# A post-norm attention and channel-mix block: GpSimd's bias sum split per block, and every engine's step in another order

## The chip, the cores and the metric

The kernel runs on one core of a Trainium2 chip. The metric is the device time of one execution in microseconds, taken from repeated runs; the profile is one execution recorded by the hardware profiler. The engines are named PE (TensorE, matrix products and transposes), DVE (VectorE), ACT (ScalarE), POOL (GpSimd) and SP (SyncE, here only the queue that issues DMAs). Each runs its own instructions strictly in the order of the program and waits on semaphores that the others raise.

## The reference

One sequence of 4096 tokens of 256 features goes through two layers, each followed by a layer norm without gain:

```python
# attention: 16 heads of 16 features, 4 key/value groups, each query sees itself and the 127 tokens before it
q = x @ Wq + bq;  k = x @ Wk + bk;  v = x @ Wv + bv          # k, v: 4 groups x 16
scores = where(i - 128 >= j or i < j, -1e9, q @ k.T / sqrt(16))
x = layernorm(x + softmax(scores) @ v @ Wo + bo)
# channel mix: every token is mixed with the one before it
xr = mu_r * x + (1 - mu_r) * x_prev;  xk = mu_k * x + (1 - mu_k) * x_prev
x = layernorm(x + sigmoid(xr @ W_r.T) * (relu(xk @ W_k.T) ** 2 @ W_v.T))
```

## The kernel before

The tokens are cut into 32 blocks of 128, and four blocks make a superblock (8 of them). Projections are made per superblock: three chunks of 128 columns (chunk 0 holds k and v, chunks 1 and 2 hold q; L893), split by ACT, DVE and POOL into three bf16 parts (high, middle, low: L517, L528, L402; rest: L677), spilled to DRAM by SP and loaded back with the parts stacked along the contraction (ks, qs: L312 to L329). v is turned by four transposes (L908) and copied to vals (L686).

The rest goes by blocks. For block t+1, DVE copies qs to query tiles (tile_q, L696), PE computes scores of tiles only to find their row maxima (six groups, "max 0 to 5", L943 and L952), DVE reduces them (L704), casts and transposes them (turn_max, L711 to L718), and SP writes them into two extra rows of qs (L336), so that the real scores come out with the maximum taken off. For block t, PE makes eight score products of 128x512 ("score 0 to 7", L969) into two PSUM banks, ACT takes their exponentials (L535), POOL zeroes what the window excludes (mask, L410). PE multiplies by the values (L983), turns the result back (L1040), DVE normalises (L808, L814), PE turns it again (L1048) and applies Wo (output product, L1081). DVE adds x + bo from x_bo and takes the moments (first residual, L830, L723 to L728), POOL raises the variance to -1/2 and forms the shift (root, L417, L419), ACT applies the norm (L582). PE turns x2 (L1032), ACT copies it (L592), POOL forms the difference of neighbouring tokens (L470), DVE makes two pairs of mixes (L780), PE the r product (L1059) and the k product (L1070), ACT tanh, relu and square (L598, L603, L609), PE the second product (L1024), DVE the gate (L789) and the second residual with its moments (L799), POOL the second root, ACT the second norm (L617), SP the store (L342).

All this is a software pipeline: in step t (block j = t mod 4 of superblock s) each engine works on several blocks at once, in an order written out by hand in its function `step`, which `run` calls. In step t, PE computes the maxima of t+1, the scores of t, the values and attention transposes of t-1, the output product and turn of x2 of t-2, the r and k products of t-3, the second product of t-4. Projections of superblock s+2 begin in the step with j = 3 (chunks 0 and 1) and go on as those of s+1 in the steps with j = 0 (chunk 2) and j = 1 (turn of v).

x_bo holds x + bo for two superblocks. It is made by POOL from x_in, loaded by SP, in one instruction per superblock of 128x1024 elements (L396), for superblocks 2 to 7 in the step with j = 2, between masks 2 and 3:

```python
                nc.gpsimd.tensor_tensor(x_bo[:, par], x_in[:, par],
                                        bo_b.unsqueeze(1).to_broadcast([P, SB_BLKS, D]), ALU.add).then_inc(s_xbo, 1)
```

## Time and profile before

| | us |
|---|---|
| median of 3 runs | 454.38 (453.68 to 455.26) |
| the profiled execution, its own time: the span from its first to its last instruction | 449.1 |
| TensorE busy in it | 407.7 |
| VectorE busy | 344.6 |
| ScalarE busy | 272.8 |
| GpSimd busy | 291.2 |

The busy times are sums of the durations of one engine's instructions, so an engine at 91% may still not be the cause of the other 9%. The span is that of one recorded execution; the runs are timed apart from it, from outside, and come out a few microseconds longer. DMA runs beside all this on 16 engines and moves 39.25 MB.

### The profile page before, as it was taken

The page shows a single profiled execution, that of the slowest core. Times are in us where ns is not written, and L with a number is a line of the kernel's source. Part 1 is how long each engine was busy: PE and PEld are TensorE (multiplying, and loading weights), DVE is VectorE, ACT ScalarE, POOL GpSimd, SP SyncE. Part 2 cuts the span into 40 slices and gives each one's busy share as a digit, 9 for nine tenths or more (in the row PEclk, how much of TensorE's full clock was granted, in tenths as well). Part 3 has the DMA queues.
Part 4 walks back from the last instruction along what each step waited for, and adds up shares of the span by engine and source line. Part 5 has one row for each costly group of instructions (what it writes and reads, how often), then busy time and mean ns, then how long its engine had stood idle before and what let it go on. Part 6 is the DMA issues. An engine that isn't in the chain of part 4 may idle for free.

```text
span 449.1 us, 8432 instructions
## 1 busy us (share of the span) xinstructions
PE 407.7 (91%) x2542; PEld 251.9 (56%) x2542; DVE 344.6 (77%) x852; ACT 272.8 (61%) x566; POOL 291.2 (65%) x466
## 2 busy tenths in 40 slices
PE   8976999997999979997999979997999979999853
PEld 3444546664556656564556665564656656665532
DVE  5765775898678976899688986799878988996551
ACT  2512567775667747764677657666577657778522
POOL 4552666776487856677487766688487767876531
PEclk9986899998999989999999989999999989999995
DMA  8484585412733175321753146421823144000000
GB/s 324 115 141 91 134 148 138 100 49 46 140 101 84 50 94 146 82 66 43 110 163 86 49 74 152 87 60 47 120 65 94 49 62 70 14 13 27 12 23 23
DMA packets 50892, 39.25 MB, mean 87 GB/s; under 512 B 33696, under 2 KB 42400, under 8 KB 50720
## 3 DMA queue, kind: packets, MB, share of 16 engines
q1 hardware_dynamic: 50416, 37.93, 38.9%
q10 hardware_dynamic: 432, 0.79, 0.6%
q8 instruction: 20, 0.33, 0.3%
q14 instruction: 24, 0.20, 0.2%
HBM read 26.38 MB, written 12.06 MB: 86 GB/s over the span
## 4 chain that ended last, share of the span: by engine, by line
PE 64%; DVE 19%; ACT 6%; issue 6%; DMA 2%; POOL 1%; SPq 1%; ACTq 0%; DVEq 0%; POOLq 0%
PE av_ps L983 11%; PE score_ps L969 9%; PE proj_ps L893 8%; PE max_ps L952 6%; PE gen L1070 6%; PE gen L1024 6%; PE gen L1081 5%; PE gen L1059 4%; DVE neg_max L704 4%; DVE q_tiles L696 3%; DVE max_parts L711 3%; PE max_ps L943 3%; ACT parts L517 2%; DVE mix L780 2%; PE av_ps L1040 2%
## 5 line engine op out<-in xcount | busy, mean ns | idle before, releaser
L410 POOL TENSOR_SCALAR_AFFINE_SELECT probs<-probs 128x512 f32<-128x512 f32 x252 | 168.2, 678 | 108.0 <-ACT probs L535 105.7
L535 ACT ACTIVATE probs<-score_ps 128x512 f32<-128x512 f32 x252 | 148.4, 598 | 86.0 <-PE score_ps L969 85.6
L969 PE MATMUL score_ps<-qs,ks 98*128 98x512 bf16 x252 | 99.8, 398 | 2.2 <-ACT probs L535 1.4
L704 DVE TENSOR_REDUCE neg_max<-max_ps 128x3 f32<-128x480 f32 x144 | 87.4, 631 | 12.3 <-PE max_ps L952 12.1
L983 PE MATMUL av_ps<-probs,vals 128*32 128x512 f32 x504 | 67.0, 605 | 0.9 <-POOL probs L410 0.8
L969 PEld LDWEIGHTS score_ps<-qs,ks 98*128 98x128 bf16 x252 | 25.0, 100 | 57.3 <-ACT probs L535 47.9
L1070 PE MATMUL gen<-mix,rest_w 128*128 128x128 f32 x256 | 38.7, 299 | 16.9 <-DVE mix L780 15.5
L952 PE MATMUL max_ps<-ks,q_tiles 96*128 96x160 bf16 x416 | 52.3, 243 | 0.0
L417 POOL TENSOR_TENSOR rstd<-var,minus_half 128x1 f32<-128x1 f32 x64 | 35.7, 558 | 21.7 <-DVE var L728 20.8
L1070 PEld LDWEIGHTS gen<-mix,rest_w 128*128 128x128 f32 x256 | 35.4, 208 | 22.7 <-DVE mix L780 17.8
L780 DVE SCALAR_TENSOR_TENSOR mix<-diff,first,x_t 128x128 f32<-128x128 f32 x128 | 43.8, 385 | 0.0
L952 PEld LDWEIGHTS max_ps<-ks,q_tiles 96*128 96x128 bf16 x416 | 37.9, 103 | 8.2 <-issue 1.9
L677 DVE SCALAR_TENSOR_TENSOR rest<-proj_ps,first,parts 128x512 f32<-128x512 f32 x19 | 14.3, 751 | 35.5 <-ACT parts L517 32.4
L893 PE MATMUL proj_ps<-x_t,first 128*128 128x512 f32 x76 | 38.3, 628 | 0.7 <-DMA first<-w_first 0.7
L943 PE MATMUL max_ps<-edge_mask,ident_b 128*128 128x192 bf16 x138 | 35.2, 255 | 3.2 <-issue 2.1
L1024 PE MATMUL gen<-rest_w,act_k 128*128 128x256 f32 x128 | 35.9, 405 | 2.1 <-ACT act_k L609 2.0
L402 POOL TENSOR_TENSOR parts<-rest,parts 128x512 bf16<-128x512 f32 x24 | 30.7, 1282 | 10.5 <-ACT parts L528 10.5
L1059 PE MATMUL gen<-rest_w,mix 128*128 128x256 f32 x128 | 34.3, 390 | 3.0 <-DVE mix L780 3.0
L1081 PE MATMUL gen<-rest_w,att_c 128*128 128x256 f32 x128 | 32.9, 379 | 0.0
L696 DVE COPY q_tiles<-qs 96x2048 bf16<-96x2048 bf16 x32 | 27.3, 853 | 5.0 <-DMA qs<-q_parts 5.0
L603 ACT ACTIVATE relu_k<-gen 128x256 f32<-128x256 f32 x32 | 12.7, 397 | 29.8 <-PE gen L1070 29.8
L582 ACT ACTIVATE x<-y,shift,rstd 128x256 f32<-128x256 f32 x32 | 19.2, 599 | 17.4 <-POOL shift L419 16.6
(86 smaller groups left out, 663.2 us busy)
## 6 DMA issues: line engine op xcount, KB each, us to landing
qs<-q_parts SPq DMA_DIRECT2D x48, 192.0 KB, 6.1
q_parts<-parts SPq DMA_DIRECT2D x48, 128.0 KB, 2.2
x_t<-x_feat SPq DMA_DIRECT2D x8, 512.0 KB, 3.7
x_in<-x_nat SPq DMA_DIRECT2D x8, 512.0 KB, 4.5
out<-out_t SPq DMA_DIRECT2D x32, 128.0 KB, 2.0
ks<-k_parts SPq DMA_DIRECT2D x42, 80.0 KB, 2.9
qs<-q_parts SPq DMA_DIRECT2D x42, 64.0 KB, 2.2
k_parts<-parts SPq DMA_DIRECT2D x8, 192.0 KB, 2.8
```

Source lines behind the costliest of these rows:

```text
L410: nc.gpsimd.affine_select(out=v, in_=v, compare_op=ALU.is_ge if i % 2 else ALU.is_gt, fill=0.0, base=0, pattern=[[0, HPG], [sign, BLK]], c ...
L535: nc.scalar.activation(probs[:, buf, i], score_ps[i % 2][:, :], ACT.Exp, scale=SCALE).then_inc(s_exp, 1)
L704: nc.vector.tensor_reduce(neg_max[:, TPB * i:TPB * i + n], max_bank(t, j, i)[:, 0:n * TILE_KEYS].rearrange("p (n k) -> p n k", k=TILE_KEYS ...
L780: nc.vector.scalar_tensor_tensor(out=mix[:, w, c], in0=diff[:, c], scalar=small_cols[:, MU_COL + w * DC + c:MU_COL + w * DC + c + 1], in1= ...
L893: ins = nc.tensor.matmul((ps or proj_ps)[:, 0:SB], wqkv[:, c, m * P:(m + 1) * P], x_t[:, par, c], start=(c == 0), stop=(c == DC - 1))
L952: ins = nc.tensor.matmul(dst, q_tiles[:, j % 2, tile], ks[0:ROWS, par, g, k0:k0 + TILE_KEYS], start=False, stop=(k == len(tiles) - 1), ski ...
L969: nc.tensor.matmul(score_ps[i % 2][:, :].rearrange("p (h q) -> p h q", q=BLK), ks[0:ROWS + MPARTS, par, g, k0:k0 + BLK], qs[0:ROWS + MPART ...
L983: ins = nc.tensor.matmul(av_ps[g * VCOL:(g + 1) * VCOL, :], vals[:, pk, jk, g, :], probs[:, j % 2, 2 * g + half], start=(half == 0 or not ...
L1024: ins = nc.tensor.matmul(gen0[:, 0:D], act_k[:, c], w_t[:, 2, c], start=(c == 0), stop=(c == DC - 1))
L1059: ins = nc.tensor.matmul(gen0[:, 0:D], mix[:, 0, c], w_t[:, 0, c], start=(c == 0), stop=(c == DC - 1))
L1070: ins = nc.tensor.matmul(gen0[:, o * BLK:(o + 1) * BLK], w_t[:, 1, c, o * P:(o + 1) * P], mix[:, 1, c], start=(c == 0), stop=(c == DC - 1))
L1081: ins = nc.tensor.matmul(gen1[:, 0:D], att_c[:, c], wo[:, c], start=(c == 0), stop=(c == DC - 1))
```

## The change

The sum of x and bo is made per block, in 128x256 elements, one a step, into a ring of four blocks (x_bo[:, t % 4]). It waits until the first residual of the block four before has read its place, and the load of x_in waits for the sums of its superblock's blocks. `run`, `superblock` and the `step` functions are replaced by one loop over t for each engine, unrolled for all 32 blocks and a few steps of drain, with the same operations in another order; `on(u)` is true for blocks that exist, `ahead(u)` where u is the first block of a superblock from 2 on (or from 1 on). The waits between operations are the same or follow from the new order (tanh, square and tile_q have one more wait each, on things done long before; PE's waits for free PSUM banks are written anew). The small tensors of the two norms are put together in pairs.

```diff
-        x_bo = sb("x_bo", [P, 2, SB_BLKS, D])
+        x_bo = sb("x_bo", [P, 4, D])
...
@@ sync: the loop (the start issues the same transfers as before)
+            for t in range(NBLK + 6):
+                if on(t - 6):
+                    store(t - 6)
+                if ahead(t + 1, 1):
+                    stack_q((t + 1) // SB_BLKS, 1, SB_BLKS, s_stack)
+                if ahead(t + 4, 1):
+                    spill_k((t + 4) // SB_BLKS)
+                if ahead(t + 2, 1):
+                    stack_q((t + 2) // SB_BLKS, 0, 1, s_stack0)
+                if ahead(t + 5):
+                    load_nat((t + 5) // SB_BLKS)
+                if ahead(t + 6):
+                    load_feat((t + 6) // SB_BLKS)
+                if ahead(t + 4, 1):
+                    stack_k((t + 4) // SB_BLKS)
+                if 1 <= t + 1 < NBLK:
+                    max_in(t + 1)
+                if ahead(t + 4, 1):
+                    spill_q((t + 4) // SB_BLKS, 0)
+                    spill_q((t + 4) // SB_BLKS, 1)
...
@@ gpsimd
-            def x_plus_bo(s, par):
-                if later(s, 2):
-                    pool.wait_ge(s_y1, (s - 1) * SB_BLKS)
-                pool.wait_ge(s_x[par], loaded(s, par))
-                nc.gpsimd.tensor_tensor(x_bo[:, par], x_in[:, par],
-                                        bo_b.unsqueeze(1).to_broadcast([P, SB_BLKS, D]), ALU.add).then_inc(s_xbo, 1)
+        def _(pool):
+            def x_plus_bo(t):
+                if t >= 4:
+                    pool.wait_ge(s_y1, t - 4 + 1)
+                pool.wait_ge(s_x[t // SB_BLKS % 2], loaded(t // SB_BLKS))
+                nc.gpsimd.tensor_tensor(x_bo[:, t % 4], x_in[:, t // SB_BLKS % 2, t % SB_BLKS], bo_b,
+                                        ALU.add).then_inc(s_xbo, 1)
...
+            for t in range(NBLK + 5):
+                if on(t - 1):
+                    mask(t - 1, 7)
+                if on(t - 3):
+                    difference(t - 3)
+                if on(t - 5):
+                    root(t - 5, 1)
+                if 2 <= t + 1 < NBLK:
+                    x_plus_bo(t + 1)
+                if ahead(t + 3):
+                    low_part((t + 3) // SB_BLKS, 2)
+                if on(t):
+                    mask(t, 0)
+                if on(t - 2):
+                    root(t - 2, 0)
+                if on(t):
+                    mask(t, 3)
+                    mask(t, 2)
+                    mask(t, 1)
+                    mask(t, 4)
+                if ahead(t + 5):
+                    low_part((t + 5) // SB_BLKS, 0)
+                if ahead(t + 4):
+                    low_part((t + 4) // SB_BLKS, 1)
+                if on(t):
+                    mask(t, 5)
+                    mask(t, 6)
@@ scalar: the loop
+            for t in range(NBLK + 5):
+                if on(t - 2):
+                    att_c_copy(t - 2)
+                if on(t - 1):
+                    exps(t - 1, 7)
+                if on(t):
+                    exps(t, 0)
+                if ahead(t + 5):
+                    high_part((t + 5) // SB_BLKS, 0)
+                if ahead(t + 3):
+                    middle_part((t + 3) // SB_BLKS, 2)
+                if on(t):
+                    exps(t, 1)
+                    exps(t, 2)
+                if ahead(t + 4):
+                    middle_part((t + 4) // SB_BLKS, 1)
+                if on(t - 5):
+                    second_norm(t - 5)
+                if on(t - 1):
+                    att_t_copy(t - 1)
+                if on(t - 3):
+                    tanh(t - 3)
+                if on(t):
+                    exps(t, 3)
+                if on(t - 2):
+                    first_norm(t - 2)
+                if on(t):
+                    exps(t, 4)
+                if ahead(t + 4):
+                    high_part((t + 4) // SB_BLKS, 2)
+                if ahead(t + 5):
+                    middle_part((t + 5) // SB_BLKS, 0)
+                if on(t - 3):
+                    relu(t - 3)
+                if on(t):
+                    exps(t, 5)
+                if on(t - 3):
+                    square(t - 3)
+                if ahead(t + 5):
+                    high_part((t + 5) // SB_BLKS, 1)
+                if on(t):
+                    exps(t, 6)
+                if on(t - 2):
+                    x2_t_copy(t - 2)
@@ vector: the loop
+            for t in range(-1, NBLK + 5):
+                if 1 <= t + 1 < NBLK:
+                    tile_max(t + 1, 1)
+                if on(t - 5):
+                    second_moments(t - 5)
+                if 1 <= t + 1 < NBLK:
+                    tile_max(t + 1, 2)
+                    tile_max(t + 1, 3)
+                if on(t - 3):
+                    mixed(t - 3, 0)
+                if 1 <= t + 1 < NBLK:
+                    tile_max(t + 1, 4)
+                if on(t - 4):
+                    gate(t - 4)
+                if on(t - 2):
+                    first_residual(t - 2)
+                    token_before(t - 2)
+                if 1 <= t + 1 < NBLK:
+                    tile_max(t + 1, 5)
+                if on(t - 2):
+                    first_moments(t - 2)
+                if 1 <= t + 1 < NBLK:
+                    turn_max(t + 1)
+                if on(t - 3):
+                    mixed(t - 3, 1)
+                if on(t - 4):
+                    second_residual(t - 4)
+                if ahead(t + 5):
+                    rest_part((t + 5) // SB_BLKS, 0)
+                if 2 <= t + 2 < NBLK:
+                    tile_q(t + 2)
+                if on(t - 1):
+                    normalise(t - 1)
+                if ahead(t + 4):
+                    rest_part((t + 4) // SB_BLKS, 2)
+                if 1 <= t + 2 < NBLK:
+                    tile_max(t + 2, 0)
+                if ahead(t + 5):
+                    rest_part((t + 5) // SB_BLKS, 1)
+                if ahead(t + 3):
+                    val_copy((t + 3) // SB_BLKS)
@@ tensor: the loop
+            for t in range(NBLK + 4):
+                if ahead(t + 2):
+                    v_turn((t + 2) // SB_BLKS)
+                if on(t - 1):
+                    score(t - 1, 4)
+                if on(t - 2):
+                    turn_back(t - 2)
+                if ahead(t + 3):
+                    project_chunk((t + 3) // SB_BLKS, 2)
+                if on(t - 4):
+                    k_product(t - 4)
+                if on(t - 1):
+                    score(t - 1, 5)
+                if 1 <= t + 1 < NBLK:
+                    max_scores(t + 1, 0)
+                if ahead(t + 4):
+                    project_chunk((t + 4) // SB_BLKS, 1)
+                if 1 <= t + 1 < NBLK:
+                    max_scores(t + 1, 1)
+                if on(t - 3):
+                    turn_x2(t - 3)
+                if on(t - 1):
+                    score(t - 1, 6)
+                if on(t - 2):
+                    turn_attention(t - 2)
+                if on(t - 1):
+                    score(t - 1, 7)
+                if on(t - 4):
+                    second_product(t - 4)
+                if 1 <= t + 1 < NBLK:
+                    max_scores(t + 1, 2)
+                    max_scores(t + 1, 3)
+                if ahead(t + 5):
+                    project_chunk((t + 5) // SB_BLKS, 0)
+                if on(t):
+                    score(t, 0)
+                if on(t - 2):
+                    output_product(t - 2)
+                if 1 <= t + 1 < NBLK:
+                    max_scores(t + 1, 4)
+                if on(t):
+                    score(t, 1)
+                if 1 <= t + 1 < NBLK:
+                    max_scores(t + 1, 5)
+                if on(t):
+                    score(t, 2)
+                if on(t - 1):
+                    values(t - 1, 0)
+                    values(t - 1, 1)
+                if on(t - 3):
+                    r_product(t - 3)
+                if on(t):
+                    score(t, 3)
```

## Rows read from the trace of the kernel before

**Rows 1.** The page: busy us and share by engine; granted clock in 40 slices.

```profile
PE 407.7 (91%) x2542; PEld 251.9 (56%) x2542; DVE 344.6 (77%) x852; ACT 272.8 (61%) x566; POOL 291.2 (65%) x466
...
PEclk9986899998999989999999989999999989999995
```

**Rows 2.** Windows: stretch and length, busy us (instructions) by engine, clock, DMA.

```profile
378.88:388.80 9.92, 9.92 (x77) 6.79 (x75) 9.08 (x26) 7.63 (x18) 7.73 (x13) 1.00 0.05 14
...
215.61:229.62 14.01, 13.90 (x86) 8.18 (x83) 9.84 (x27) 9.51 (x21) 8.98 (x16) 1.00 0.66 143
...
229.62:241.97 12.35, 12.05 (x81) 7.32 (x79) 10.28 (x24) 8.89 (x20) 8.78 (x14) 1.00 0.42 90
...
241.97:252.61 10.64, 10.64 (x81) 7.23 (x79) 9.78 (x27) 7.19 (x16) 8.17 (x14) 1.00 0.24 61
...
252.61:267.10 14.49, 11.78 (x78) 7.88 (x75) 12.53 (x30) 8.14 (x20) 9.89 (x15) 0.88 0.28 62
...
304.12:317.17 13.05, 10.36 (x77) 6.62 (x75) 12.43 (x30) 7.62 (x18) 9.55 (x14) 1.00 0.21 52
...
97.34:368.89 271.55, 253.14 (x1638) 159.85 (x1635) 224.68 (x555) 178.55 (x375) 190.66 (x296) 0.97 0.41 87
```

**Rows 3.** Timeline, 256 to 268 us: start, us, instruction, [idle before, releaser].

```profile
258.86 2.36 POOL L396 TENSOR_TENSOR x_bo<-x_in,rest_w 128x1024 f32<-128x1024 f32 x1
...
258.97 2.29 DVE L711 CAST max_parts<-neg_max 128x16 bf16<-128x16 f32 x1
...
263.23 2.07 PE L1070 MATMUL gen<-mix,rest_w 128*128 128x128 f32 x8 [2.58 <-DVE mix L780]
```

**Rows 4.** Single lines: count, duration in ns min/median/max, first and last start.

```profile
L396 POOL TENSOR_TENSOR x_bo<-x_in,rest_w x8: 2347/2355/2362, 16.8 to 360.4; 128x1024 f32<-128x1024 f32 x8
...
L470 POOL TENSOR_TENSOR diff<-x_t x32: 607/612/613, 61.6 to 434.5; 128x256 f32<-128x256 f32 x32
...
L711 DVE CAST max_parts<-neg_max x32: 178/240/2285, 32.5 to 404.8; 128x16 bf16<-128x16 f32 x32
...
L799 DVE SCALAR_TENSOR_TENSOR y<-gated,x x32: 414/844/1375, 86.0 to 444.1; 128x256 f32<-128x256 f32 x32
```

**Rows 5.** Timeline, 282 to 300 us: GpSimd and VectorE at once.

```profile
285.16 1.16 POOL L402 TENSOR_TENSOR parts<-rest,parts 128x512 bf16<-128x512 f32 x1
...
285.18 0.65 DVE L704 TENSOR_REDUCE neg_max<-max_ps 128x3 f32<-128x480 f32 x1
```

**Rows 6.** Timeline, 372 to 386 us: statistics, norm, and what follows it.

```profile
382.12 0.43 DVE L723 BATCH_NORM_STATS2 stats<-y 128x6 f32<-128x256 f32 x1
...
384.19 0.60 ACT L582 ACTIVATE x<-y,shift,rstd 128x256 f32<-128x256 f32 x1
...
384.70 0.56 ACT L567 COPY att_t<-av_ps 128x512 f32<-128x512 f32 x1
```

**Rows 7.** Groups of the whole span: busy us, mean ns | idle before, releaser.

```profile
L410 POOL TENSOR_SCALAR_AFFINE_SELECT probs<-probs 128x512 f32<-128x512 f32 x252 | 168.2, 678 | 108.0 <-ACT probs L535 105.7
...
L535 ACT ACTIVATE probs<-score_ps 128x512 f32<-128x512 f32 x252 | 148.4, 598 | 86.0 <-PE score_ps L969 85.6
...
L704 DVE TENSOR_REDUCE neg_max<-max_ps 128x3 f32<-128x480 f32 x144 | 87.4, 631 | 12.3 <-PE max_ps L952 12.1
...
L780 DVE SCALAR_TENSOR_TENSOR mix<-diff,first,x_t 128x128 f32<-128x128 f32 x128 | 43.8, 385 | 0.0
...
L609 ACT ACTIVATE act_k<-relu_k 128x256 f32<-128x256 f32 x32 | 13.3, 417 | 1.0
...
L572 ACT COPY att_c<-av_ps 128x256 f32<-128x256 f32 x32 | 11.6, 364 | 0.0
```

**Rows 8.** The chain that ended last, in order: start, us, what.

```profile
272.84 1.93 PE proj_ps L893 x4
```

**Rows 9.** Issues of the q stack for blocks 1 to 3, and their landing.

```profile
L327 SPq DMA_DIRECT2D qs<-q_parts x90: 302/428/1258, 25.8 to 367.4; - x90
...
DMA to landing us min/median/max: 2.1/3.7/8.9
```

More of the change, by code:

```diff
@@ L381, in tail @@
-            def tail():
-                for buf in range(2):
-                    sp.wait_ge(s_store[buf], 16 * (NBLK // 2) + 1)
-                    sp.nop(nofuse=True)
-            run(sp, start, step, tail)
+                sp.dma_start(out_blk[t], out_t[:, t % 2]).then_inc(s_store[t % 2], 16)
+            load_feat(0)
+            load_nat(0)
+            sp.dma_start(rest_w[:, :], w_rest).then_inc(s_restw, 16)
+            load_feat(1)
+            load_nat(1)
+            spill_k(0)
+            spill_q(0, 0)
@@ L870, in _ @@
-            run(dve, start, step)
+            zeros()
+            identities()
+            rest_part(0, 0)
+            rest_part(0, 1)
+            rest_part(0, 2)
+            val_copy(0)
+            masks()
+            rest_part(1, 0)
+            rest_part(1, 1)
+            rest_part(1, 2)
+            val_copy(1)
+            tile_q(0)
+            tile_max(0, 0)
+            tile_max(0, 1)
+            tile_max(0, 2)
+            tile_max(0, 3)
+            tile_max(0, 4)
+            tile_max(0, 5)
@@ new lines, in turn_attention, with r_product @@
+            def turn_attention(t):
+                pe.wait_ge(s_att, t + 1)
+                for c in range(DC):
+                    ins = nc.tensor.transpose(av_ps[:, c * BLK:(c + 1) * BLK], att[:, c * P:(c + 1) * P],
+                                              ident[:, :])
+                ins.then_inc(s_ctr, 1)
+            def r_product(t):
+                pe.wait_ge(s_mix, t * 4 + 2)
+                if t:
+                    pe.wait_ge(s_gated, t)
+                for c in range(DC):
+                    ins = nc.tensor.matmul(gen0[:, 0:D], mix[:, 0, c], w_t[:, 0, c], start=(c == 0),
+                                           stop=(c == DC - 1))
+                ins.then_inc(s_r, 1)
@@ new lines, in k_product, with output_product @@
+            def k_product(t):
+                pe.wait_ge(s_mix, t * 4 + 4)
+                pe.wait_ge(s_tanh, t + 1)
+                for o in range(DC):
+                    for c in range(DC):
+                        ins = nc.tensor.matmul(gen0[:, o * BLK:(o + 1) * BLK], w_t[:, 1, c, o * P:(o + 1) * P],
+                                               mix[:, 1, c], start=(c == 0), stop=(c == DC - 1))
+                ins.then_inc(s_k, 1)
+            def output_product(t):
+                pe.wait_ge(s_att_c, t + 1)
+                if t:
+                    pe.wait_ge(s_x2t, t)
+                for c in range(DC):
+                    ins = nc.tensor.matmul(gen1[:, 0:D], att_c[:, c], wo[:, c], start=(c == 0),
+                                           stop=(c == DC - 1))
+                ins.then_inc(s_wo_ps, 1)
```

912 lines of the change are left out of this document (350 added, 562 removed).

## The prediction

> **What bounds the kernel now.** I read the profiled execution, whose span is 449.1 us; the median of the runs shown, 454.4 us, stands 5.3 us above it, and those 5.3 us are added at the end. First the page's busy shares and its clock line: TensorE 91%, VectorE 77%, GpSimd 65%, ScalarE 61%, and a TensorE clock that is 9 nearly everywhere and dips to 8 now and then [rows 1]. 91% says "TensorE", the dips say "something stops it now and then", so the second view is the busy time step by step (from the start of one second product of the channel mix, L1024, to the next). The reader is to see three kinds of step [rows 2]. A plain step takes 9.92 us and TensorE is busy all of it, VectorE for 9.08, ScalarE for 7.63, GpSimd for 7.73. Steps with projection work take 14.01, 12.35 and 10.64 us, TensorE busy for all but 0.3 us at most. And the step with j = 2 takes 14.49 us although it has no projection work: TensorE is idle for 2.7 us of it and the granted clock falls to 0.88; one of them keeps its clock and takes 13.05.
>
> The third view, the timeline inside such a step, says why [rows 3]. GpSimd starts the sum of x and bo for a whole superblock (L396, 2.36 us) at 258.86. VectorE's next instruction is the cast of the row maxima (L711), started at 258.97, and it ends only when the sum does, after 2.29 us. Behind it in VectorE's order stand the rest of the maxima's transposition and the second pair of mixes, and the k product on TensorE waits for those, 2.58 us idle. Then TensorE starts at its lower level: eight pieces take 2.07 us. The cast takes 0.178 us at its shortest and 2.285 at its longest, the sum 2.35 us every time [rows 4].
>
> So: a pipeline at TensorE's 9.92 us a step, with one stop in each of six superblocks (1 to 6).
>
> **The sum of x and bo.** It goes from 8 instructions of 128x1024 to 32 of 128x256. The difference of neighbouring tokens (L470) is a GpSimd instruction of two operands of just that shape and takes 0.61 us [rows 4]. 4 x 0.61 = 2.44 us for a superblock against 2.36: nothing for GpSimd. What changes is the longest time for which it can hold VectorE up, 0.61 instead of 2.3 us. The stop's worth: the 21 steps from 97.34 to 368.89 are five of each projection kind and six with j = 2, 271.55 - 5 x (14.01 + 12.35 + 10.64) = 86.55; less 6 x 9.92 = 59.5 it is 27.0 us [rows 2]. If the small sums block nothing, all of it goes. Next late behind the k product would be TensorE's own queue, which is full, so no other wait takes the stop's place at once. Upper bound of what the small sums cost: each delays VectorE by 0.61 us and the delay goes whole to TensorE, in the 24 steps of the six superblocks, 14.6 us. Lower bound: 0. In the new order the sum stands behind the difference and the second root, when VectorE is about at a maximum from PSUM, the gate and the first residual. The nearest row is the low part of a projection (L402), on GpSimd over a maximum (L704): the maximum still takes 0.65 us [rows 5]. I take 0.
>
> The Trainium skill (SBUF — State Buffer, "Who interferes with whom") has it that the port pair that VectorE and GpSimd share is locked for a whole instruction, that the second to issue waits for all of it, and that VectorE's instructions with two SBUF inputs are hit as well as its fast copies and casts. The casts of 2.29 us agree. By that rule splitting frees no port time, and it speaks for the first rival below, which is priced from rows.
>
> **The order of the steps.** Counted through the loops, every engine issues what it issued before, so the busy times of a plain step stay. What moves: scores 4 to 7 of a block go over TensorE's step border, exponential 7 and mask 7 over those of ScalarE and GpSimd; on TensorE the transposes of the attention and of x2 and the k product go one step later; maximum 0 of the next block but one is taken at the end of VectorE's step. The question is whether the in-order queues still close in 9.9 us. The longest loop I find goes from one block's exponential 7 to the next one's: mask 7, the difference, the first pair of mixes, maximum 4, gate, first residual, maximum 5, the moments and the root, first norm, exponential 4, relu, exponential 5, square, exponential 6, the copies of x2 and of the attention, exponential 7. In numbers: four exponentials of 0.60 (2.40), the mask 0.68, the difference 0.61, two mixes of 0.385 (0.77), two maxima of 0.63 (1.26), six instructions of 256 columns (gate, residual, relu, square, two copies) of 0.36 to 0.42, at 0.40 (2.40), 2.07 from the start of the statistics to that of the norm, the norm 0.60 [rows 4, 6, 7]. Together 10.8 us. These are full durations; independent neighbours on an engine overlap: the norm of 384.19 takes 0.60 and the next one starts after 0.51 [rows 6]. With 0.09 us for each of 14 such neighbours the loop takes 9.5. Bounds 9.5 and 10.8 against TensorE's 9.92; I take 9.92, since the overlap has a row, so the cost is 0. The cover is thin, though: a first norm that waits now holds exponentials 4 and 5, and through them scores 6 and 7. At 10.8 the 27 steps from block 5 on would cost 0.88 x 27 = 24 us.
>
> In the steps with projection work the excess over 9.92 is 4.09 + 2.43 + 0.72 = 7.2 us a superblock. TensorE's own part are three chunks, the first of them 1.93 us and the others 1.7 [rows 8], and the turn of v, four transposes, 0.6: 6.0 us. The other 1.2 are waits for PSUM and for copies. In the new order the chunks start in three steps instead of two with more work between, and maxima 2 and 3 come behind scores and the second product instead of close behind 0 and 1. I take half back, 0.6 x 6 = 3.7 us; the ends are 0 and 7.5.
>
> **SyncE and its transfers.** Loads, stores, spills and stacks change places in SyncE's order. The tightest is the q stack of blocks 1 to 3, now behind the maxima's rows of block 3: six issues of 0.43 us, landing within 8.9 us at worst [rows 9], 11.5 us together, and the copy to q tiles that needs it stands some 13 us behind the first issue (one step of 9.9, the first chunk's 1.9, and about one more of the step before). Hidden, by 1.5 us. The second q spill of a superblock now waits for a low part one step later; queued behind it are a store and the next rows of maxima, which are due 1 to 2 us after: no cost.
>
> **Start and end.** The two big sums at the start shrink by 3.5 us together, but block 0 waits there for the q stacks: 0. The last 30 us are the chain of one block, with the same operations in the same sequence: 0, give or take 2.
>
> Sum: 449.1 - 27.0 - 3.7 = 418.4, and 5.3 make 423.7: **424 us**. This case's own range is 417 to 430 (projection waits 0 or 7.5 us back, thin cover 0 or 0.2 us a step).
>
> **Rivals.**
> 1. VectorE's block comes back in small: each new sum meets a cast, the copy of q tiles or an instruction of two SBUF operands. For it: the second residual (L799) takes 0.41 us at its shortest and 0.84 in the median [rows 4]. Against it: where the sum stands in the order, and the 0.84 us that VectorE has free in a plain step. Price 14.6 us: 439 us.
> 2. The loop rules, mildly: half-way between 9.92 and 10.8, 10.36 us a step, 12 us: 436 us. For it the sum of full durations, against it the overlap.
> 3. The loop rules and the kernel gets slower. One mechanism: the first norm of block t-2, which stands before exponential 4 on ScalarE, waits for GpSimd's first root, and that for VectorE's moments behind maximum 5, for which TensorE must have issued its maxima first; so scores 6 and 7 wait on late work of TensorE itself. It decides from the point where 27 steps lose the 30.7 us gained, 9.92 + 1.14 = 11.06 us a step. Full durations and 0.17 us of wait at three handoffs make 11.3: 27 x 1.38 = 37 us, 449.1 - 30.7 + 37.3 + 5.3 = 461 us. Against: today's step has nearly the same links and closes in 9.92.
> 4. TensorE isn't at its limit at 9.92, and a better order runs down to VectorE's 9.08 plus gaps, about 9.4: 27 x 0.5 = 14 us less, 410 us. For it: weight loads fill only 6.79 of the 9.92 us. Against it: no idle time at all [rows 2]. The Trainium skill (Perfetto Trace Analysis, "Identifying the Most-Contended Engine") calls matmul busy time a bad measure of the room left and asks for weight-load busy time; that rule is for this rival.
> 5. It doesn't do what it says: the big stop goes, but the q stack lands late instead, its 1.5 us of cover being gone; 3 us of wait and 1.5 of lower clock in six superblocks, 27 us: 451 us.
>
> **Chances.** Forecast 0.60, rival 1 0.13, rival 2 0.09, rival 3 0.09, rival 4 0.06, rival 5 0.03. About 0.3% is what a measurement of this kernel can tell from no change. Rivals 1, 2 and 4 are faster, rival 3 is slower, of rival 5 two thirds are no change; with a little for mishaps elsewhere: faster 0.87, same 0.03, slower 0.10. The range, 415 to 440, takes in the forecast and rivals 1 and 2, 0.82.
>
> **What would show it.** The cast's longest duration falls from 2.29 to under 0.8 us; 32 sums of about 0.61; no step of 13 to 15 us without projection work; TensorE busy 95% or more between the first and the last block, with no dips in the clock there; plain steps of 9.7 to 10.1 us. The prediction is wrong if plain steps take over 10.3 us with scores that wait for exponentials (rivals 2 and 3), if casts and q tile copies are long beside the new sums (rival 1), or if a copy to q tiles waits for a DMA (rival 5).

## The result

The changed kernel takes 412.5 us (median of 4 executions, 409.1 to 413.4) against 454.6 us for the kernel before (453.7 to 455.3): a ratio of 0.908, 95% interval 0.901 to 0.914. The direction was forecast, the size was not: 424.0 us and the range of 415 to 440 both lie above it. In a later job the two had a ratio of 0.913 (0.895 to 0.930). Medians and ranges in this document hold every execution; ratios leave out those that stand over 1.5% above the fastest of their kernel.

**The profile after.** The page first: busy us and share by engine, the clock line, and the shares of the chain of work that ended last.

```profile
PE 382.1 (93%) x2542; PEld 247.2 (60%) x2542; DVE 304.3 (74%) x852; ACT 268.7 (65%) x566; POOL 295.6 (72%) x490
...
PEclk9997799999999999999999999999999998999998
...
PE 56%; DMA 17%; DVE 10%; SPq 7%; issue 4%; ACT 3%; POOL 2%; ACTq 0%; POOLq 0%; DVEq 0%
```

The dips of [rows 1] in the middle of the clock line are gone. New is "DMA 17%" in the chain (2% before): a transfer is now part of what sets the end. VectorE's busy time fell by 40 us with the same 852 instructions; the cast (19.3 us in all before, 7.3 now) and the second residual (25.3 and 13.4) are 24 of them.

Windows by kind of step (from one second product of the channel mix, now L923, to the next; columns as in [rows 2]):

```profile
72.46:83.91 11.45, 11.45 (x80) 7.57 (x78) 10.01 (x25) 8.23 (x18) 7.96 (x12) 1.00 0.32 62
83.91:94.08 10.17, 10.17 (x79) 7.28 (x78) 8.67 (x27) 7.92 (x18) 9.56 (x16) 1.00 0.38 92
94.08:103.81 9.73, 9.73 (x75) 6.73 (x74) 8.95 (x28) 7.34 (x17) 7.99 (x15) 1.00 0.42 117
...
148.89:164.37 15.48, 13.41 (x83) 8.14 (x83) 9.30 (x27) 9.55 (x21) 10.70 (x17) 1.00 0.82 131
195.89:210.19 14.30, 13.41 (x83) 8.14 (x82) 9.50 (x27) 9.55 (x21) 10.61 (x17) 1.00 0.76 122
356.59:366.32 9.73, 9.73 (x76) 6.81 (x75) 8.36 (x26) 7.33 (x17) 8.36 (x15) 1.00 0.05 16
375.94:410.90 34.96, 24.87 (x139) 15.80 (x138) 16.50 (x57) 17.71 (x40) 16.62 (x34) 0.97 0.07 23
```

The step with j = 2 (third row) is now a plain step. Plain steps take 9.73 us, the stretch with chunk 2 of a projection 11.45 and the one with the turn of v 10.17 (before 12.35 and 10.64), TensorE busy all through. Chunks 0 and 1 both lie in the stretch from the second product of the step with j = 3 to the next, as before the change. Only that one did not get shorter: 13.72 to 15.48 us (before 14.01, one of them 14.48), with TensorE idle for up to 2.07 of them.

Single lines, as in [rows 4]: the small sum, the cast, the second residual, the copy of the q tiles.

```profile
L334 POOL TENSOR_TENSOR x_bo<-x_in,rest_w x32: 724/732/1071, 16.4 to 369.9; 128x256 f32<-128x256 f32 x32
...
L651 DVE CAST max_parts<-neg_max x32: 168/170/476, 30.3 to 372.2; 128x16 bf16<-128x16 f32 x32
...
L699 DVE SCALAR_TENSOR_TENSOR y<-gated,x x32: 417/418/426, 79.9 to 405.9; 128x256 f32<-128x256 f32 x32
...
L638 DVE COPY q_tiles<-qs x32: 645/683/1123, 25.2 to 363.6; 96x2048 bf16<-96x2048 bf16 x32
```

The cast's longest fell from 2.29 us to 0.48, the second residual from 0.84 in the median (1.38 at its longest) to 0.418, with 0.426 at its longest. The small sum takes 0.73 us, not the 0.61 of the forecast, so four of them are 2.93 us against 2.36 for the whole one.

Now the wait that came instead. VectorE's waits (us in total, times, longest), and the chain that ended last through one step with j = 3 (start, us, what):

```profile
DVE q_tiles L638 <- DMA qs<-q_parts: 16.2, 9, 5.6
```

```profile
147.56 1.48 SPq L274
...
149.09 0.42 SPq L274
...
150.97 9.16 DMA qs<-q_parts
...
160.16 0.93 DVE q_tiles L638
...
161.14 0.26 PE max_ps L875
```

SyncE issues the q stack of blocks 1 to 3 from 147.56 on, the last piece lands 12.6 us after that, and VectorE's copy, which had been free to start at 158.07, waits 2.09 us for it; TensorE's next maximum waits behind the copy.

**Where the 38.2 us of span went** (449.1 less 410.9), by stretches of equal work from the starts of the second products: the start, 1.9; the first two steps with projection work behind it, 1.4; the 21 steps of [rows 2]'s last row, 271.55 less 238.81 = 32.7 (six with j = 2: 27.4; ten with j = 0 and 1: 6.9; five with j = 3: 1.6 *lost*); the next four, 3.7 *lost* (12.93 and 10.77 among them, the last stack); everything from 375.94 on, 40.83 less 34.96 = 5.9.

### The profile page after: what moved, and what is told of

Read it like the earlier page. It is cut to its first block, busy times and chain, and to the rows that moved or that the text cites. A ratio compares the mean times of both kernels' runs of the same rounds, so it can differ in the third digit from the quotient of the medians.

```text
span 410.9 us, 8541 instructions
## 1 busy us (share of the span) xinstructions
PE 382.1 (93%) x2542; PEld 247.2 (60%) x2542; DVE 304.3 (74%) x852; ACT 268.7 (65%) x566; POOL 295.6 (72%) x490
## 4 chain that ended last, share of the span: by engine, by line
PE 56%; DMA 17%; DVE 10%; SPq 7%; issue 4%; ACT 3%; POOL 2%; ACTq 0%; POOLq 0%; DVEq 0%
DMA qs<-q_parts 15%; PE score_ps L901 8%; PE av_ps L914 7%; PE proj_ps L827 6%; PE max_ps L884 5%; PE gen L923 5%; PE gen L973 5%; SPq L274 4%; PE gen L954 4%; PE gen L963 4%; PE max_ps L875 2%; DVE neg_max L645 2%; SPq L282 2%; DVE q_tiles L638 2%; PE av_ps L937 2%
## 5 line engine op out<-in xcount | busy, mean ns | idle before, releaser
L350 POOL TENSOR_SCALAR_AFFINE_SELECT probs<-probs 128x512 f32<-128x512 f32 x252 | 162.2, 669 | 46.1 <-ACT probs L474 45.0
L901 PE MATMUL score_ps<-qs,ks 98*128 98x512 bf16 x252 | 91.7, 387 | 1.4 <-ACT probs L474 1.3
L914 PE MATMUL av_ps<-probs,vals 128*32 128x512 f32 x504 | 60.7, 598 | 0.3 <-POOL probs L350 0.2
L682 DVE SCALAR_TENSOR_TENSOR mix<-diff,first,x_t 128x128 f32<-128x128 f32 x128 | 40.7, 359 | 16.4 <-POOL diff L372 16.4
L954 PEld LDWEIGHTS gen<-rest_w,mix 128*128 128x128 f32 x128 | 21.7, 189 | 28.5 <-issue 24.3
L340 POOL TENSOR_TENSOR parts<-rest,parts 128x512 bf16<-128x512 f32 x24 | 28.7, 1199 | 11.7 <-ACT parts L465 11.7
L923 PE MATMUL gen<-rest_w,act_k 128*128 128x256 f32 x128 | 34.1, 389 | 1.8 <-ACT act_k L519 1.8
L963 PE MATMUL gen<-mix,rest_w 128*128 128x128 f32 x256 | 34.2, 276 | 1.6 <-DVE mix L682 0.9
L638 DVE COPY q_tiles<-qs 96x2048 bf16<-96x2048 bf16 x32 | 23.3, 729 | 16.2 <-DMA qs<-q_parts 16.2
L963 PEld LDWEIGHTS gen<-mix,rest_w 128*128 128x128 f32 x256 | 31.5, 191 | 5.7 <-issue 3.8
L360 POOL TENSOR_SCALAR shift<-mv,rstd 128x1 f32<-128x1 f32 x64 | 27.0, 421 | 6.3
```

The source lines that it names most:

```text
L350: nc.gpsimd.affine_select(out=v, in_=v, compare_op=ALU.is_ge if i % 2 else ALU.is_gt, fill=0.0, base=0, pattern=[[0, HPG], [sign, BLK]], c ...
L901: nc.tensor.matmul(score_ps[i % 2][:, :].rearrange("p (h q) -> p h q", q=BLK), ks[0:ROWS + MPARTS, s % 2, g, k0:k0 + BLK], qs[0:ROWS + MPA ...
L914: ins = nc.tensor.matmul(av_ps[g * VCOL:(g + 1) * VCOL, :], vals[:, b // SB_BLKS % 2, b % SB_BLKS, g, :], probs[:, t % 2, 2 * g + half], s ...
L923: ins = nc.tensor.matmul(gen0[:, 0:D], act_k[:, c], w_t[:, 2, c], start=(c == 0), stop=(c == DC - 1))
L954: ins = nc.tensor.matmul(gen0[:, 0:D], mix[:, 0, c], w_t[:, 0, c], start=(c == 0), stop=(c == DC - 1))
L963: ins = nc.tensor.matmul(gen0[:, o * BLK:(o + 1) * BLK], w_t[:, 1, c, o * P:(o + 1) * P], mix[:, 1, c], start=(c == 0), stop=(c == DC - 1))
```

## The experiments

**Was it the split or the order?** Three kernels. First the kernel before with nothing but the split, in the step with j = 2:

```diff
                 if ahead and j == 2:
-                    x_plus_bo(s + 1, 1 - par)
+                    x_plus_bo_block(s + 1, 1 - par, 0)
                 if scores:
                     mask(t, 3, j % 2)
+                if ahead and j == 2:
+                    x_plus_bo_block(s + 1, 1 - par, 1)
...
```

> The kernel before, with only the sum split: four sums of 128x256 instead of one of 128x1024, after masks 2, 3, 4 and 5 of the step with j = 2. Theory A (the length of one GpSimd instruction makes the stop): VectorE is held for 0.6 us at most at a time, most of the 27 us of the six stops goes, 428 to 433 us. Theory B (where the sum stands makes the stop, the port is held as long in all): the four sums meet the cast, the mixes and the copy of q tiles one after the other, 442 to 452 us.

Measured: 436.8 us (432.3 to 439.1), ratio 0.959 (0.949 to 0.969), between the two. The mechanism is theory B's, at a lower price: the small sums meet the cast, the mixes and the copy of the q tiles one after the other, and the cast and the copy are held up by 0.5 us each.

```profile
249.12 0.65 DVE L725 CAST max_parts<-neg_max 128x16 bf16<-128x16 f32 x1
...
252.05 0.72 POOL L403 TENSOR_TENSOR x_bo<-x_in,rest_w 128x256 f32<-128x256 f32 x1
252.13 1.20 DVE L710 COPY q_tiles<-qs 96x2048 bf16<-96x2048 bf16 x1
```

Then the kernel before with the whole sum, only moved:

```diff
-                if ahead and j == 2:
-                    x_plus_bo(s + 1, 1 - par)
                 if scores:
                     mask(t, 3, j % 2)
...
                 if f3:
                     difference(t - 3)
+                if ahead and j == 2:
+                    x_plus_bo(s + 1, 1 - par)
```

> The kernel before, with only the place of the big sum changed: from behind mask 2 to behind the difference, at the start of GpSimd's step. Theory A: the sum still holds VectorE for up to 2.3 us at its next instruction with two SBUF inputs or fast cast, and masks 0 and 1, the root and the first norm come 2.4 us late: 445 to 460 us. Theory B: VectorE is then at maxima, the gate and the first residual, which read PSUM; the cast is back at 0.2 us and 15 to 27 us go: 428 to 440 us.

Measured: 436.5 us (435.9 to 437.4), ratio 0.962 (0.954 to 0.969): the same gain without a split, and in the range of theory B. Last the new order with the sum whole again:

```diff
-                if 2 <= t + 1 < NBLK:
-                    x_plus_bo(t + 1)
+                if ahead(t + 1):
+                    x_plus_bo((t + 1) // SB_BLKS)
```

> The kernel after, with the sum of x and bo made whole again (128x1024, once a superblock, in the place of its first quarter). Theory A: the stop comes back, six times 4.5 us, 435 to 442 us. Theory B: in the new order the sum stands 3.4 us ahead of the cast, beside maxima, gate and residual from PSUM, and costs next to nothing: 411 to 417 us.

Measured: 408.5 us (407.5 to 410.3), ratio 0.902 (0.893 to 0.910), not slower than the change with its split (0.908): theory A is out. Windows of the step with j = 2 with the split alone and with the move alone:

```profile
242.77:254.10 11.33, 10.37 (x77) 6.63 (x75) 10.87 (x26) 7.64 (x18) 10.17 (x17) 1.00 0.25 63
```

```profile
98.38:110.32 11.94, 10.65 (x78) 6.58 (x75) 10.34 (x27) 7.41 (x18) 10.21 (x14) 1.00 0.29 66
```

and in the new order with the whole sum, the step with j = 3 that now holds it, the sum with its neighbours on VectorE, and the cast over the whole span:

```profile
237.33:251.06 13.73, 13.43 (x84) 8.15 (x83) 9.15 (x27) 9.56 (x21) 12.03 (x17) 1.00 0.80 135
```

```profile
240.90 2.36 POOL L333 TENSOR_TENSOR x_bo<-x_in,rest_w 128x1024 f32<-128x1024 f32 x1
242.12 0.66 DVE L644 TENSOR_REDUCE neg_max<-max_ps 128x3 f32<-128x480 f32 x1 [1.40 <-PE max_ps L883]
242.69 0.41 DVE L689 SCALAR_TENSOR_TENSOR gated<-tanh_r,gen 128x256 f32<-128x256 f32 x1
```

```profile
L650 DVE CAST max_parts<-neg_max x32: 168/170/409, 30.1 to 367.0; 128x16 bf16<-128x16 f32 x32
```

The reader is to see that the sum lasts 2.36 us as ever, and that VectorE meanwhile waits for TensorE and then takes a maximum and the gate out of PSUM, at their usual 0.66 and 0.41 us. So the stop was a matter of what stands beside the sum.

Splitting it or moving it each take more than half of it away in the old order: 14.5 us to 11.3 or 11.9, not to 9.9. About 1.5 us of that is clock (14.5 against the 13.05 of the step that kept it), which fell to 0.88 or 0.91 in five of these six steps before the change and is 1.00 in all of them in both experiments. What is left has two different causes. With the split it is the sums that VectorE still meets, shown above, and the step behind, with j = 3, grows from 14.01 to 14.66 in four of five cases. With the move the cast takes 0.18 us again, but GpSimd's own list is late: masks 0 and 1 and the first root stand behind the 2.36 us, the root starts 6.5 us into the step instead of 4.5, ScalarE's first norm waits for its shift, and TensorE for the copy behind the norm.

```profile
105.90 0.60 ACT L582 ACTIVATE x<-y,shift,rstd 128x256 f32<-128x256 f32 x1 [2.02 <-POOL shift L419]
...
107.02 0.66 PE L1040 MATMUL av_ps<-ident,att_t 128*128 128x128 f32 x4 [1.16 <-ACT att_t L567]
```

A long instruction on GpSimd thus has two prices, one at VectorE's next SBUF work and one in its own list. In the new order, where the whole sum falls into a step that has projection work for TensorE, neither shows (13.73 us there, the change has 13.72 to 15.48), and the split gains nothing.

**How far does the kernel before vary, and what stands around a span?** The kernel before once more, unchanged.

> The kernel before, unchanged, to read span and time of the same execution. If the 5.3 us between the profiled span and the timed median are a fixed cost around the span, every execution shows about 5 us between its time and its span. If the profiled execution of before was only a quick one, every execution shows some 1.8 us (as the kernel after does: 412.74 us with a span of 410.9) and the usual span of before is about 452.6 us.

Measured: 456.0 us (450.4 to 462.0, 10 executions), ratio 0.999 (0.993 to 1.005). In every execution the time stood 1.7 to 1.8 us above its span, while the span went from 448.6 to 460.3; the mean granted clock lay between 0.930 and 0.944, lowest in the longest execution, but it does not order the others (0.943 at 448.6, 0.944 at 456.0). So the 5.3 us that the prediction added were not something around the span: the profiled execution was a quick one.

**Is the plain step's 0.19 us the order or one pair of instructions?** In the change TensorE's two halves of the values product follow each other; this kernel puts score 2 and a maximum between them, as before.

```diff
-                if 1 <= t + 1 < NBLK:
-                    max_scores(t + 1, 5)
-                if on(t):
-                    score(t, 2)
                 if on(t - 1):
                     values(t - 1, 0)
+                if on(t):
+                    score(t, 2)
+                if 1 <= t + 1 < NBLK:
+                    max_scores(t + 1, 5)
+                if on(t - 1):
                     values(t - 1, 1)
```

> The changed kernel, with TensorE's two halves of the values product taken apart again: score 2 and the sixth maxima product stand between them, as before the change. Theory H (the plain step fell from 9.92 to 9.73 because two halves side by side take 1.85 us where halves apart took 1.99 us): the plain step rises to 9.83 to 9.90, the median by 3 to 5 us, to 415.5 to 417.5. Theory I (the 0.19 us is the sum of many small waits that the whole order removed): the plain step stays within 0.05 us of 9.73 and the median within 1.5 us of the changed kernel's.

Measured: 414.3 us (413.4 to 415.6), ratio 0.909 (0.905 to 0.913). The window of a plain step, and TensorE's timeline through the place:

```profile
347.13:357.10 9.97, 9.97 (x75) 6.72 (x74) 8.44 (x26) 7.44 (x17) 7.39 (x13) 1.00 0.05 15
```

```profile
349.95 0.38 PE L901 MATMUL score_ps<-qs,ks 98*128 98x512 bf16 x1
350.26 1.07 PE L914 MATMUL av_ps<-probs,vals 128*32 128x512 f32 x8
351.26 0.39 PE L901 MATMUL score_ps<-qs,ks 98*128 98x512 bf16 x1
351.49 0.20 PE L875 MATMUL proj_ps<-edge_mask,ident_b 128*128 128x64 bf16 x1
...
351.68 1.06 PE L914 MATMUL av_ps<-probs,vals 128*32 128x512 f32 x8
352.68 1.13 PE L954 MATMUL gen<-rest_w,mix 128*128 128x256 f32 x4
```

The same in the changed kernel:

```profile
153.47 0.38 PE L901 MATMUL score_ps<-qs,ks 98*128 98x512 bf16 x1
153.69 0.19 PE L875 MATMUL max_ps<-edge_mask,ident_b 128*128 128x64 bf16 x1
...
153.79 0.38 PE L901 MATMUL score_ps<-qs,ks 98*128 98x512 bf16 x1
154.10 1.92 PE L914 MATMUL av_ps<-probs,vals 128*32 128x512 f32 x16
155.96 1.13 PE L954 MATMUL gen<-rest_w,mix 128*128 128x256 f32 x4
```

Both stretches hold two scores, one short maximum and the two halves. From start to start they take 2.73 us (349.95 to 352.68) and 2.49 (153.47 to 155.96). The halves take 1.00 each when apart and 1.86 together (0.14 us). The rest is what stands right ahead of a half: it takes 0.09 us longer than elsewhere (a score 0.31 against 0.22, the short maximum 0.19 against 0.10), once when the halves are together and twice when they are apart (0.10). The plain step went from 9.73 to 9.97, more than theory H had for it, so this one pair is worth the whole 0.19 us and theory I is out. Theory H is wrong about the median: 0.24 us in 27 steps are 6.5 us, and 1.8 showed in the median. In the profile the five steps with j = 3 take 68.9 us instead of 72.1 and the two behind the last stack 22.2 instead of 23.7: a later TensorE hides more of the q stack.

**The late q stack.** First it was issued a step earlier, together with block 0's, at the head of SyncE's list.

```diff
-                if ahead(t + 1, 1):
-                    stack_q((t + 1) // SB_BLKS, 1, SB_BLKS, s_stack)
...
                 if ahead(t + 2, 1):
                     stack_q((t + 2) // SB_BLKS, 0, 1, s_stack0)
+                    stack_q((t + 2) // SB_BLKS, 1, SB_BLKS, s_stack)
```

> The kernel after, with SyncE issuing the q stack of blocks 1 to 3 one step earlier, right behind that of block 0. Theory C (the late stack, my fifth rival, takes part of the gain): the steps that make chunk 0 fall from 14.3 to 13.4 us and the last one from 12.9 to 9.8, some 8 us in all: 403 to 406 us. Theory D (the stack is late only on paper; TensorE would wait there for something else, as the transposes of the step): 409 to 414 us. Against C could also be that the rows of maxima queue behind the longer stack on SyncE and scores wait.

Measured: 443.5 us (438.5 to 448.9), ratio 0.968 (0.938 to 0.998): by the ratios some 25 us worse than the change in the same job (0.913, below), which neither theory had. The trace is of the slowest of its four executions. TensorE's waits, a window of a step with j = 3, and the load of x_feat among the issues (KB each, us to landing):

```profile
PE proj_ps L826 <- DMA x_t<-x_feat: 26.1, 6, 6.8
```

```profile
162.32:181.90 19.58, 16.38 (x83) 9.54 (x83) 9.04 (x27) 9.66 (x21) 10.13 (x17) 0.83 0.34 82
```

```profile
x_t<-x_feat SPq DMA_DIRECT2D x8, 512.0 KB, 9.4
```

That load landed after 4.1 us in the change; now it is issued behind twelve pieces of stack (six of 64 KB, six of 192 KB) and lands after 9.4, and the first chunk of the projection waits up to 6.8 us for it, after which TensorE runs at a lower granted clock (0.83 over that step). The same with the whole sum:

> The kernel after with both: the sum of x and bo whole again, and the q stack of blocks 1 to 3 one step earlier. If splitting costs what the last comparison seemed to show (3 to 4 us) and the late stack some 8, this is the fastest of all: 398 to 403 us. If splitting is neutral, it stands level with the early stack alone, within 1.5 us.

Measured: 431.6 us (426.2 to 438.7), steps with j = 3 of 16.3 to 18.9 us, 20.3 us of waits for x_feat. So the two do not stand level: here the split costs 12 us in the median. The two traces suggest how, though no run separates it. In the step with j = 1 a small sum stands ahead of GpSimd's low part of chunk 2, which starts 4.26 us into the step instead of 3.57. SyncE's second q spill, the stacks and the load of x_feat follow it, so the six waits for x_feat are 1 us longer in the mean (26.1 us against 20.3 in all), and the granted clock falls to 0.83 in four of five steps with j = 3; with the whole sum it stays at 1.00 in four of them. The change once more, in the same job:

> The kernel after, unchanged, to stand beside the next two on one chip: 409 to 414 us by all theories.

Measured: 415.6 us (three executions of 412.4 to 416.3 and one of 493.1 at a mean granted clock of 0.75), ratio 0.913 (0.895 to 0.930).

What was still to be told apart: whether the stack's place in the list cost that, or its traffic. So it was put behind the other transfers of the same step.

```diff
-                if ahead(t + 1, 1):
-                    stack_q((t + 1) // SB_BLKS, 1, SB_BLKS, s_stack)
...
                 if 1 <= t + 1 < NBLK:
                     max_in(t + 1)
+                if ahead(t + 2, 1):
+                    stack_q((t + 2) // SB_BLKS, 1, SB_BLKS, s_stack)
```

> The changed kernel, with the load of the q stack's blocks 1 to 3 moved from the head of SyncE's list in the step with j = 3 to the end of its list in the step with j = 2, behind the loads of x_nat and x_feat and behind the load of the maxima. Theory F (moving the stack to j = 2 cost what it did only because it then stood ahead of the x_feat load, which TensorE waited for 26.1 us in six super-blocks): x_feat lands as in the changed kernel (about 4 us), the stack is there before the copies of j = 3, the steps with j = 3 fall from 14.3 to about 13.4, and the median falls by 5 to 8 us, to 404 to 408. Theory G (what costs is the stack's transfer itself while the projections run, wherever it stands in the list): j = 3 steps stay at 14.3 or grow, 412 or more.

> The same move of the q stack's load in the new order with the whole sum of 128x2048 once in a super-block. Theory F: 3 to 6 us below the 408.5 of that kernel without the move, so 402 to 406; steps with j = 3 at 13.0 to 13.4. Theory G: 408 or more.

(The whole sum is 128x1024, as above.) Measured: 405.3 us (403.2 to 408.1), ratio 0.890 (0.884 to 0.895), and with the whole sum 404.5 us (403.6 to 405.1), ratio 0.887 (0.883 to 0.891). Both beat the kernel before and the change (0.908, 0.901 to 0.914), and with the stack in this place the split is worth nothing either way. Theory F holds. Of the latter the page's clock line, its x_feat load, and a window of a step with j = 3:

```profile
PEclk9998899999999999999999999999999999999998
```

```profile
x_t<-x_feat SPq DMA_DIRECT2D x8, 512.0 KB, 3.6
```

```profile
236.99:250.24 13.25, 13.25 (x84) 8.23 (x83) 9.04 (x27) 9.55 (x21) 11.55 (x17) 1.00 0.75 133
```

TensorE is busy all of the step, which is 0.76 us shorter than before the change. In the change the stack's first issue comes 2.12 us after VectorE has transposed the row maxima, here 1.49 us, since one store fewer stands ahead of it: a mere 0.6 us sooner. The five steps with j = 3 take 68.3 us instead of 72.1 without the whole sum, 66.7 with it; that was enough in most steps, not in all (one without the whole sum still takes 14.31). The load of x_in stays behind the stack, in the step with j = 3, and lands after 9.3 us, as in the change (9.2); no engine waits for it.

**Does the small sum's place matter?** The changed kernel with the sum behind root 0, beside VectorE's second residual and copy of the q tiles.

```diff
-                if 2 <= t + 1 < NBLK:
-                    x_plus_bo(t + 1)
...
                 if on(t - 2):
                     root(t - 2, 0)
+                if 2 <= t + 1 < NBLK:
+                    x_plus_bo(t + 1)
```

> The changed kernel, with the small sum of each block moved three places down GpSimd's list, from behind root 1 (where VectorE runs operations that read PSUM) to behind root 0 (where VectorE runs the second residual of 128x256 and the copy of the q tiles, which work in SBUF alone). Theory M (a sum of 128x256 holds up only SBUF work that meets it, each time by less than its own 0.72 us, and TensorE, busy for the whole of a plain step, hides that): the second residual or the q tile copy gets 0.3 to 0.6 us longer, the plain step stays at 9.73 and the median within 2 us of the changed kernel's. Theory N (the good place of the sum is what makes the new order fast): the plain step rises by 0.3 us or more and the median by 8 us or more.

Measured: 408.2 us (407.3 to 410.2), ratio 0.902 (0.893 to 0.911), the plain step at 9.73. The median is 4.2 us below the change's, which was measured in another job; the intervals of the ratios overlap. The sum and the copy it meets:

```profile
L334 POOL TENSOR_TENSOR x_bo<-x_in,rest_w x32: 722/1172/1177, 16.5 to 371.1; 128x256 f32<-128x256 f32 x32
...
L638 DVE COPY q_tiles<-qs x32: 646/683/1182, 25.3 to 360.8; 96x2048 bf16<-96x2048 bf16 x32
```

Theory M is right on the step and half wrong on how: the one that gets longer (0.73 to 1.17 us) is the sum, which starts 0.09 us after the copy (360.87 and 360.78), while the copy keeps its 0.683. In the old order it was the cast, which started 0.11 us after the sum [rows 3]. The Trainium skill (SBUF — State Buffer, "Who interferes with whom") has the second to issue wait for the first. Both cases agree in who waits; how long fits for the cast (it ends 0.04 us after the sum) and roughly for the sum (0.44 us longer, with 0.59 us of the copy still to run).

**The tail.** The kernel before with idle matmuls in the drain steps; they write a score bank that nothing reads any more (TensorE first waits until its last exponentials are taken; three more stand ahead of the k product).

```diff
+                drain = t > NBLK
+                def fill(n):
+                    if drain:
+                        keep_running(score_ps[0], n)
...
+                fill(6)
                 if f4:
                     second_product(t - 4)
...
+                fill(4)
                 if f3:
                     r_product(t - 3)
...
```

> The kernel before, with idle matmuls between the products of the drain steps (t over 32), which keep TensorE busy where it ran out of work and its granted clock fell to the lower level from about 436 us on. They add nothing to the result. Theory J (the changed kernel's gain of 5.9 us behind step 31 is partly this clock: three products at 2.07, 1.64 and 2.05 us instead of about 1.1): the tail's products take 1.1 to 1.2 us and the median falls by 2 to 4 us. Theory K (the tail waits for VectorE and ScalarE, and the clock matters little): within 1 us of the kernel before, or slower.

Measured: 449.8 us (447.9 to 451.6), ratio 0.986 (0.980 to 0.993). The windows from the same product to the end, of the kernel before in its repetition and of this one:

```profile
408.75:451.90 43.15, 30.31 (x138) 18.64 (x138) 17.56 (x60) 17.39 (x40) 16.75 (x32) 0.76 0.06 19
```

```profile
408.95:448.60 39.65, 35.75 (x190) 20.58 (x190) 17.58 (x60) 17.41 (x40) 16.79 (x32) 1.00 0.06 21
```

3.5 us less with the clock at its upper level throughout, which is theory J in the profile; the 5.8 us of the medians (3.4 to 9.2 by the interval) are no contradiction, and more than the tail is not claimed.

## Why the prediction was too high

- **Offset.** "Those 5.3 us are added at the end" was the first step to fail. 1.8 us stand around the span; the rest was the profiled execution's luck. That is 3.5 us of the 11.5 by which the forecast was too high.
- **"The stop's worth ... 27.0 us."** Right in size and in place: the steps with j = 2 lost 27.4 (the forecast's subtraction took all five steps with j = 3 at 14.01, one was 14.48, so 26.5 were there to lose, and the shorter plain step gave the rest). The reason was half right. The cast did stand behind the sum, but "what changes is the longest time for which it can hold VectorE up" was the wrong half: in the new order the whole sum costs nothing either. The sum's cost of 0 was right for its place, not for its length, and the length itself was off (0.73 us each, not 0.61).
- **"I take 9.92".** This failed, and it put at nothing a gain that the order brought: 9.73. Operations and counts were the same, but TensorE's plain step was not a constant: two halves that follow each other save 0.24 us by the experiment. Over 27 steps 9.92 to 9.73 is 5.1 us. Rival 4 had said that the step would get shorter, and by weight loads that leave room; it got 0.19 us, not the 0.5 that rival 4 priced, and busy time stayed 100%. The thin cover of the long loop held in every step, so rivals 2 and 3 did not occur.
- **Projection work, "I take half back, 3.7 us".** Too low: with the stack in time the excess over a plain step is 1.72 + 0.44 + 3.52 = 5.7 us a super-block (11.45, 10.17, 13.25 less 9.73) against 7.2, so 1.56 x 6 = 9.4 us, beyond the upper end of 7.5; "TensorE's own part", 6.0, was itself too high. What gave back the 1.56 was not taken apart; it was not that chunks 0 and 1 lie in different steps, since the stretch with j = 3 holds both before and after.
- **"Hidden, by 1.5 us."** This failed the other way. Six issues and the last landing took 12.6 us instead of 11.5 (the first issue alone took 1.48 us instead of 0.43, the last piece landed after 9.16), and the copy was due 10.5 us after the first issue, not 13. Before the change it was due after 14.1:

```profile
263.37 2.89 SPq L327 DMA_DIRECT2D qs<-q_parts  x6
...
277.43 0.68 DVE L696 COPY q_tiles<-qs 96x2048 bf16<-96x2048 bf16 x1
```

Of the 3.6 us that went, 2.4 are the copy's new place (1.70 us behind the start of its step's transposition of maxima instead of 4.08), 0.6 the stack's (2.12 us behind the one before instead of 1.50), and 0.55 the shorter time between the two transpositions (10.93 us, 11.48 before). So the order took the cover, not the shorter step. It was short by 2.1 us in that step, and cost 5.9 us in five steps with j = 3 (72.1 less 5 x 13.25) and 4.2 in the two behind them. Rival 5 had the mechanism with a chance of 0.03; it came along with the forecast instead of in its place.
- **"Start and end, 0".** 1.9 and 5.9 us. The profile before shows the tail at a clock of 0.85 from 408.27 on; the change's is 0.97. The idle matmuls put 1.2 to 3.5 us of it on the clock (40.83 or 43.15 less 39.65). The remaining 4.7 (39.65 less 34.96) come with the order of the drain steps: argued from the windows, no experiment took it apart, nor the 1.9 us of the start.

Together, in the span: 5.1 + 5.7 + 1.9 + 5.9 more than forecast, 10 less by the stack, 0.5 less by the stop (26.5 down to 9.92): 8 against the 7.5 that the span was off. That the miss was no larger is luck: gains of 18.6 us that the forecast did not have stood against 10 that the late stack took, and with the stack in time in most steps the same order takes 405.3 us.

## What to carry to other kernels

When an instruction on one engine stalls another, look first at what stands beside it in the other's list: moving it gained as much as cutting it up. Then look at what stands behind it in its own list, which a whole instruction holds up once and small ones a little in every step. A new order takes cover away from transfers that the old one hid, so work out for each from where it is issued to where it is due in the new lists, and when one is moved forward in a shared issue list, name the load it now stands before: here the two ends of one step's list were over 30 us apart (438.5 us at the fastest and 408.1 at the slowest). Take the time around a span from several executions, not from the difference between one profile and a median.

## What the runs showed beyond that

- Two values products of eight matmuls each (128*32 by 128x512) take 2.00 us apart and 1.86 adjacent, and with the score between them a plain step of a fully busy TensorE goes from 9.73 to 9.97: the busy share can't show that.
- A 512 KB load landed after 4.1 us (median) with six 64 KB pieces ahead of it in SyncE's list, and after 9.4 with six of 192 KB ahead of it as well.
- Of two instructions on VectorE and GpSimd that meet in SBUF, in the two pairs timed here, the one that starts 0.1 us later grows, by 0.44 us (a sum behind a copy) or by 2.1 us (a cast behind a sum), the other not at all.
- With the same program, the kernel before, the span went from 448.6 to 460.3 us in ten executions; the kernel with the whole sum and the stack last, whose TensorE hardly stops, stayed within 403.6 and 405.1 us in its four executions.
